# Masked graph attention on one core: ScalarE's order of conversions and copies in the first chunk, VectorE's order at the last chunk border, and the transfers placed behind the last loads

## The reference

```python
def reference(x, adj, L0_gnn_W, L0_gnn_a):          # x 4096x128 f32, adj 4096x4096 int32 of 0 and 1
    h = relu(layernorm(x))
    Wh = h @ W                                      # W 128x128
    e = (Wh @ a1)[:, None] + (Wh @ a2)[None, :]
    e = where(e > 0, e, 0.2 * e)
    e = where(adj > 0, e, -9e15)
    attention = softmax(e, axis=1)
    return x + elu(attention @ Wh)
```

## Time and profile before

| | |
|---|---|
| median of 3 runs | 242.35 us (242.04 to 242.58) |
| the profiled execution's own time | 242.51 us |
| its span in the trace | 240.7 us |
| PE busy | 221.5 us, 92% |
| weight load of PE busy | 215.6 us, 90% |
| DVE busy | 198.9 us, 83% |
| ACT busy | 158.0 us, 66% |
| POOL busy | 81.2 us, 34% |
| read from HBM | 70.32 MB, 301 GB/s over the span |

### The profile page before, as it was taken

How to read it: one execution, slowest core, us unless ns; L and a number is a source line. 1 busy time by engine, 2 the same in 40 slices (tenths; PEclk the granted TensorE clock), 3 DMA queues, 4 the chain that set the end, 5 groups by cost and what they waited for, 6 DMA issues and landing times.

```text
span 240.7 us, 8054 instructions
## 1 busy us (share of the span) xinstructions
PE 221.5 (92%) x3608; PEld 215.6 (90%) x3608; DVE 198.9 (83%) x266; ACT 158.0 (66%) x139; POOL 81.2 (34%) x68
## 2 busy tenths in 40 slices
PE   6969999599999999999999999999974999999990
PEld 2759899599999999999999999999974999999980
DVE  4999998437876997877787988999979499989866
ACT  3698836696797887986756677788277338920033
POOL 4648036797000030699800300093000200692000
PEclk9997999999999999999999999999999799999997
DMA  7999999999699999999999999999999940011002
GB/s 225 362 385 388 386 387 386 386 368 366 224 313 416 398 409 410 410 405 407 357 291 365 364 365 367 370 371 311 324 406 406 413 188 3 3 50 43 3 0 89
DMA packets 29622, 72.93 MB, mean 303 GB/s; under 512 B 1554, under 2 KB 2068, under 8 KB 29588
## 3 DMA queue, kind: packets, MB, share of 16 engines
q1 hardware_dynamic: 21136, 49.81, 56.9%
q10 hardware_dynamic: 8452, 22.61, 25.7%
HBM read 70.32 MB, written 2.10 MB: 301 GB/s over the span
## 4 chain that ended last, share of the span: by engine, by line
PE 54%; ACT 11%; DMA 10%; DVE 9%; issue 7%; POOL 4%; ACTq 4%; DVEq 0%; POOLq 0%
PE acc L1043 15%; PE acc L1044 15%; PE acc L1045 15%; DMA raw<-in_adj_dram 9%; PE mask_t L1019 7%; ACTq L584 4%; ACT second L573 3%; DVE words L818 3%; ACT mask L555 2%; POOL second L430 2%; POOL val L433 2%; DVE stats L733 1%; DMA first<-in_x_dram 1%; PE acc L1007 1%; PE acc L998 1%
## 5 line engine op out<-in xcount | busy, mean ns | idle before, releaser
L818 DVE SCALAR_TENSOR_TENSOR words<-g_row,gq_word,mask_t 128x1024 f32<-128x1024 f32 x96 | 119.8, 1275 | 30.6 <-PE mask_t L1019 16.7
L1043 PE MATMUL acc<-val,words 128*128 128x129 f16 x744 | 128.0, 220 | 0.3 <-DVE wh_sb L759 0.3
L1045 PE MATMUL acc<-val,words 128*128 128x129 f16 x744 | 128.0, 220 | 0.0
L1044 PE MATMUL acc<-val,words 128*128 128x129 f16 x744 | 128.0, 220 | 0.0
L1043 PEld LDWEIGHTS acc<-val,words 128*128 128x128 f16 x744 | 72.8, 98 | 0.5 <-issue 0.5
L1044 PEld LDWEIGHTS acc<-val,words 128*128 128x128 f16 x744 | 72.8, 98 | 0.1
L1045 PEld LDWEIGHTS acc<-val,words 128*128 128x128 f16 x744 | 72.8, 98 | 0.0
L555 ACT ACTIVATE mask<-raw,step_bias 128x2048 uint8<-128x2048 int32 x28 | 54.7, 1995 | 23.3 <-DMA raw<-in_adj_dram 13.1
L1043 PE MATMUL acc<-first,words 128*128 128x129 f16 x256 | 45.4, 224 | 4.7 <-DVE num L826 2.6
L1044 PE MATMUL acc<-first,words 128*128 128x129 f16 x256 | 45.4, 224 | 0.0
L1045 PE MATMUL acc<-first,words 128*128 128x129 f16 x256 | 45.4, 224 | 0.0
(11 more groups left out here) (113 smaller groups left out, 227.2 us busy)
## 6 DMA issues: line engine op xcount, KB each, us to landing
raw<-in_adj_dram SPq DMA_DIRECT2D x36, 1024.0 KB, 14.3
raw<-in_adj_dram ACTq DMA_DIRECT2D x12, 1024.0 KB, 13.4
raw<-in_adj_dram SPq DMA_DIRECT2D x16, 512.0 KB, 12.9
raw<-in_adj_dram ACTq DMA_DIRECT2D x16, 512.0 KB, 15.5
first<-in_x_dram SPq DMA_DIRECT2D x8, 256.0 KB, 5.7
val<-in_x_dram SPq DMA_DIRECT2D x2, 512.0 KB, 22.8
out_dram<-first ACTq DMA_DIRECT2D x2, 512.0 KB, 11.9
out_dram<-val ACTq DMA_DIRECT2D x1, 512.0 KB, 2.6
```

The source lines that it names most:

```text
L818: nc.vector.scalar_tensor_tensor(words[:, q], g_row[:, c * CHUNK:(c + 1) * CHUNK], word, bytes_t, ALU.max, ALU.mult).then_inc(words_ready, 1)
L1043: nc.tensor.matmul(acc_tile(t), high, v[:, 0, 0:V], start=first and t % PT == 0, stop=False, skip_group_check=True)
L1044: nc.tensor.matmul(acc_tile(t), high, v[:, 1, 0:V], start=False, stop=False, skip_group_check=True)
L1045: last = nc.tensor.matmul(acc_tile(t), low, v[:, 0, 0:V], start=False, stop=False, skip_group_check=True)
```

## The change

It moves instructions in the queues of four engines and changes none of them.

```diff
 # SP
-                if at == 29:
-                    sp.wait_ge(words_free, SETS * U * BT)
-                    sp.wait_ge(val_moved, MOVES)
-                    load_rows(C - 2)
-                    load_rows(C - 1)
+            sp.wait_ge(words_free, SETS * U * BT)
+            sp.wait_ge(val_moved, MOVES)
+            load_rows(C - 2)
+            load_rows(C - 1)
 # ACT, first chunk
             to_bytes(0, 2, 0)
             to_bytes(0, 2, 1)
-            high_values(1, 0, CT)
-            to_bytes(0, 3, 0)
-            high_values(2, 0, CT)
-            to_bytes(0, 3, 1)
-            high_values(3, 0, CT)
-            for i in range(2 * (G - 1)):
+            for g in range(1, G):
+                to_bytes(0, 2 + g, 0)
+                to_bytes(0, 2 + g, 1)
+                high_values(g, 0, CT)
+            for i in range(4):
                 row_copy(1 + i // 2, i % 2)
-                to_bytes(0, 4 + i // 2, i % 2)
-            to_bytes(0, 7, 0)
-            to_bytes(0, 7, 1)
+                to_bytes(0, 6 + i // 2, i % 2)
 # ACT, the loop behind it
                     for k in range(2):
+                        if at == U:
+                            row_copy(G - 1, k)
                         to_bytes(c, u, k)
...
-                if at == 23:
+                if at == 27:
                     tail(1)
-                if at == 29:
-                    store(0)
-                    store(1)
+            store(0)
+            store(1)
 # DVE
-                        if (u, q) == (U - 1, BT - 1) and c < C - 1 and is_set(c + 1, ORDER[c + 1][0]):
-                            turn_set(c + 1, 0)
+                        if (u, q) == (0, 0) and is_set(c, ORDER[c][0]):
+                            turn_set(c, 0)
                         weights(c, u, q)
-                        if (u, q) == (0, 2):
+                        if (u, q) == (0, 0 if is_set(c, ORDER[c][0]) else 2):
                             take_sums(c - 1)
 # PE
-                    if u in (2, 3, 4) and q % 2 == 0:
-                        i = 2 * (u - 2) + q // 2
+                    if u in (3, 4, 5) and q % 2 == 0:
+                        i = 2 * (u - 3) + q // 2
```

## The result

The changed kernel takes 239.56 us in the median of its 20 executions (one of them took 1277.77 us), the kernel before 242.0 in 20 others. The ratio is 0.9915 (95% interval 0.9890 to 0.9939), a gain of 2.1 us (1.5 to 2.7); a second series gave 0.9897 (0.9847 to 0.9948). The forecast was 237.0, a gain of 5.35. The time lies at the upper end of the range, and the gain is less than half of what was forecast. The three executions of before that the forecast started from had a median of 242.35, so 0.35 us of the step down to 239.56 is their difference to the 20.

What follows compares the result with a forecast made beforehand. PE, busy 92% of the span, was taken as the bound, with the DMA right behind it. Word 2 behind the last border's turning comes at 185.15 instead of 190.5, so 242.35 - 5.35 = 237.0; range 235.0 to 239.7.

Steps and rivals of the forecast that it cites:

- both waits: Chunk 0: PE's waits of 1.53 us for ACT's bytes and 1.52 for ACT's row copy go, PE 3.05 earlier.
- a third wait: Last border: after waits of 1.5 and 0.7, PE waits 2.0 us for ACT's bytes of loads 28 and half of 29.
- The moves costed at nothing: Behind the border: rows behind load 31, ACT's stores, POOL's part of chunk 1's finish; cost nothing, bounds 0 and 1 us each way.
- the slump of 66 to 70: DMA at 243 GB/s instead of 409 for 4 us behind the dry queue; 1.6 us more if gone, left in.
- the slump goes with the gap: Rival, chance 0.17: DMA 4.6 us ahead, load 27 lands at 170.1, turning of unit 0 gains 7.05; 235.3.
- 5.35 us at that point: Last border, word 2 behind the turning of unit 0: at 185.15 instead of 190.5, giving 237.0.
- the fall of the earlier trace: Kernel before, behind the last border: clock granted 0.50 for 3.41 us, words 0 and 1 took 4.35 instead of 2.72, 1.63 lost.
- The rival of a second fall: Chance 0.25: the clock falls again behind PE's border waits, costing up to 1.63 us; 238.6.
- one lead of 2.9 us: DMA at 386 instead of 315 GB/s over 50 to 66, carried to load 27 (171.8) and load 29 (182.0); bounds 0 and 4.6.
- the loads don't follow: Rival, chance 0.11: load 27 still lands at 174.7, turning of unit 0 at 187.2, 2.4 gained; 240 to 241.5.

Runs made afterwards that it cites:

- the execution of 241.73 us: Profiled execution of the changed kernel with the turning of unit 0 behind word 2 and chunk 1's finish behind load 26; median 239.29, ratio 0.9885.
- the first chunk alone: Kernel before with only the first chunk's part (ACT's order of bytes, high values and copies, PE's spreading one unit later); ratio 0.9967, median 241.55 or 241.74.
- the finish behind load 26: Changed kernel with the finish of chunk 1 in ACT's queue behind load 26 instead of load 27; median 239.01, ratio 0.9884.
- the moves taken back: Changed kernel with chunk 1's finish back behind load 23, stores and rows behind load 29, first chunk and DVE's order kept; 239.24, ratio 0.9907.
- the failed test with 2 MB less: ACT's halves of loads 22 to 25 bring half their rows: changed kernel 242.49 us, ratio 0.9983; kernel before 245.42, ratio 1.0139.

## Why the prediction was wrong

**Right.** Chunk 0, point for point: both waits gone, load 10 issued at 54.09 (54 forecast), 3.04 gained by PE at its end (3.05). At the border, in the first profile: load 27 at 171.53 (171.8), DVE's turning at 175.51 (175.7), sums at 178.01 (178.05), PE at 178.71 (178.75), word 1 at 180.81 (180.85), and a third wait ahead of the turning of unit 0 for ACT. The moves costed at nothing cost nothing.

**Right by luck, the landing of load 27.** The prediction left the slump of 66 to 70 in, because the one at 118 to 124 stands without a dry queue. That one went: over 50 to 70 the DMA gained 2.9 and 1.7 us, the 4.6 of the rival "the slump goes with the gap". Up to 106 us it moved 384 GB/s where it had moved 367, 1.8 MB more, some 4.4 us at 409. Then it lost part of this where the layouts change: over 106 to 130 it moved 346 GB/s against 358, and in the nine other profiles with the new first chunk and all of loads 24 to 27 it was 325 to 348. Two steps that were wrong left 3.2 us in the first profile, near the 2.9 forecast, and less in the others. Why the second slump grew is open.

**Wrong, the clock, 1.63 of the 5.35.** "So the gain is 5.35 us at that point, if the clock stays full": that sum set a kernel before with the fall of the earlier trace rows in it against one after without. The rival of a second fall had 0.25 and a price of 1.6, and one of the two profiles of the changed kernel shows it; the price was right, and how often it is paid is not shown. The deeper fault is that the fall stood in the sum at all: it belongs to single executions of either kernel, and 14 of the 63 executions of the kernel before in the table have a mean clock of 0.989 and over, which leaves room for one such fall at most. Compared at equal clock, the forecast would have been 5.35 - 1.63 = 3.7.

The Trainium skill (TensorE: Matmul & The Clock Gate, section "HAM oscillation — how this bites in real kernels") makes the price of a throttled stretch half its length, 1.7 for 3.41 us; the trace agrees, with 1.63 twice.

**Wrong, the landing of load 29, 1.07.** The prediction carried one lead of 2.9 us to all landings ("first half of 29 (landed 184.91 - 2.9 = 182.0)"). Load 29 was issued at 161.17, 4.1 earlier than before, and landed at 183.25, only 1.66 earlier. The turning was at 185.31 and not at 184.25. 3.72 - 1.07 = 2.65, and two profiles at equal clock differ by 2.63. That is also the upper end of the first interval (1.5 to 2.7) and inside the second (1.3 to 3.7), so it agrees with the ratios.

**The lead is smaller in most profiles.** The landing of load 27 (the start of its bytes on ACT) in the ten profiles of kernels with the new first chunk and whole loads 24 to 27 was 171.53, 172.03, 172.12, 172.22, 172.62, 172.77, 172.82, 173.07, 174.06 and 175.53, against 174.72 and 174.65 with the old one. The last is from the execution of 241.73 us, and its row names DVE's words and not the load, so it may not be a landing. The middle is 172.7, a lead of 2.0 and not 2.9, and the first profile has the best of them. Where ACT did not wait for load 29 and PE stood waiting ahead of the turning, the turning came 12.32 behind this landing, three times of three, so a landing at 172.7 puts it at 185.0, near the 185.3 that load 29 allowed. So this moves the gain less than load 29 does. That it accounts for what the ratios (2.1 and 2.5) lie under 2.65 is argued, not shown, and within their intervals nothing has to be accounted for.

**Where the gain of chunk 0 went.** Of PE's 3.05 us, the first chunk alone brought 0.8 to the end (interval -0.3 to 1.9), because the next link at the border was the DMA's landing, whose lead was 1.65 there. With the border's part, what ends last ahead of the turning is either load 29, or load 27 with its bytes, the finish and the bytes of load 28. The rival "the loads don't follow" did not come true for load 27, which came 3.2 earlier in the first profile; for load 29 it did in part, with 1.66 of the 4.1.

Open: why load 29 landed 22.1 us after its issue where it took 19.6 before (165.31 to 184.91). It was not the rate. Between issue and landing the DMA moved 362 GB/s against 357 before, and between the landings of loads 27 and 29 408 against 404, but for 11.72 us instead of 10.19, so 4.8 MB instead of 4.1. Loads 28 and 29 hold 4.2 MB together, so 0.6 MB at least of this belonged to later loads and went ahead of load 29's last piece, 1.5 us at that rate. In the second profile of the changed kernel the two landings are 11.17 apart. In all other profiles in which ACT waited for both loads in full and no load was cut, they are 10.08 to 10.18 apart, as before: in three kernels (the first chunk alone, the finish behind load 26, and the moves taken back). None of the three has the finish behind load 27. Whether its place does this or two executions happened so is not shown. That some of the 16 engines end a stretch of mixed pieces later than others would fit this and the failed test with 2 MB less, but no view shows it.

## What to carry to other kernels

Take the fall of the granted clock in a profiled execution out of the sum before forecasting, and put its return in as a case; a wait that shrinks need not remove it. Look for falls in the whole span, not only at the place that is changed. When an engine's lead has to pass a point where a transfer ends the wait, count only the transfer's lead, and walk each later transfer by itself: the lead of the queue's bytes is not the lead of the landing. If two links end within tenths of each other ahead of the same wait, removing either shows little, and only the pair can open it.

## What the hardware showed

- The DMA moved 386 to 390 GB/s with 2 KB pieces, 407 to 413 with 4 KB, 365 with the layout of the sets, and 270 to 316 over 6 to 12 us where the layouts follow each other in the middle of the span.
- Reading half of the rows in one half of four loads took the rate of the stretch from 365 to 279 GB/s at the same DMA share of 1.06, and both kernels took longer, by some 2 (interval touching that of the changed kernel) and 3.4 us.
- A fall of TensorE's clock to 0.50 for 3.4 us behind the border cost 1.63 us in both kernels. It came behind waits of 1.8, 0.6 and 2.4 us in one execution of the changed kernel, and did not behind waits of 1.6, 0.6 and 3.0 us in another.
